# Attention with sixteen heads on one core: weighted sums two key blocks at a time, maxima from upper halves, and ScalarE's heads as straight code

## The reference

```python
xn = layernorm(x)
q = heads(xn @ q_w.T + q_b) / sqrt(16)
k = heads(xn @ k_w.T + k_b)
v = heads(xn @ v_w.T + v_b)
attn = softmax(einsum('bhqd,bhkd->bhqk', q, k))
ctx = einsum('bhqk,bhkd->bhqd', attn, v)
out = x + (merge(ctx) @ out_w.T + out_b) + ffn(xn)
```

## Time and profile before

| | |
|---|---|
| median of 3 runs | 2112.31 us (2112.14 to 2113.64) |
| the profiled execution's own time | 2113.7 us |
| its span, first to last instruction | 2111.9 us |
| mean granted TensorE clock | 0.993 |
| TensorE matmul busy | 2040.5 us (97%) |
| TensorE weight load busy | 689.0 us (33%) |
| ScalarE busy | 1939.8 us (92%) |
| VectorE busy | 319.3 us (15%) |
| DMA | 82.46 MB |

### The profile page before, as it was taken

How to read it: one execution, slowest core, us unless ns; L and a number is a source line. 1 busy time by engine, 2 the same in 40 slices (tenths; PEclk the granted TensorE clock), 3 DMA queues, 4 the chain that set the end, 5 groups by cost and what they waited for, 6 DMA issues and landing times.

```text
span 2111.9 us, 39181 instructions
## 1 busy us (share of the span) xinstructions
PE 2040.5 (97%) x13433; PEld 689.0 (33%) x13433; DVE 319.3 (15%) x798; ACT 1939.8 (92%) x2130; POOL 29.7 (1%) x53
## 2 busy tenths in 40 slices
PE   6889999999999999999999999999999999999988
PEld 4533333233333333323333333323333333223327
DVE  6531001010101001010101001010100101010106
ACT  2259999999999999999999999999999999999983
POOL 2000000000000000000000000000000000000000
PEclk9989999999999999999999999999999999999999
DMA  6960201111020211111020111112020111102022
GB/s 202 267 198 9 44 5 18 28 23 28 8 43 8 31 13 23 28 23 28 8 43 8 23 21 23 28 20 31 8 43 8 16 28 23 28 10 41 8 38 80
DMA packets 65569, 82.46 MB, mean 39 GB/s; under 512 B 9952, under 2 KB 47360, under 8 KB 62208
## 3 DMA queue, kind: packets, MB, share of 16 engines
q1 hardware_dynamic: 65472, 81.58, 18.9%
HBM read 54.79 MB, written 26.21 MB: 38 GB/s over the span
## 4 chain that ended last, share of the span: by engine, by line
PE 92%; ACT 2%; issue 2%; DMA 2%; SPq 1%; DVE 1%; ACTq 0%; DVEq 0%
PE banks L1001 47%; PE banks L988 38%; PE banks L949 2%; ACT probs L558 2%; PE banks L906 2%; PE banks L1100 1%; PE banks L917 1%; DMA k_parts<-probs 1%; PE banks L969 0%; PE banks L1084 0%; PE banks L1091 0%; DMA q_st<-q_parts 0%; PE banks L890 0%; DMA k_parts<-parts 0%; SPq L317 0%
## 5 line engine op out<-in xcount | busy, mean ns | idle before, releaser
L558 ACT ACTIVATE probs<-banks 128x1024 f32<-128x1024 f32 x2051 | 1890.0, 1282 | 33.4 <-PE banks L988 27.3
L1001 PE MATMUL banks<-probs,v_st 128*32 128x512 f32 x8192 | 1092.5, 605 | 0.0
L988 PE MATMUL banks<-q_st,k_st 50*128 50x512 f32 x4102 | 921.1, 484 | 28.8 <-ACT probs L558 25.9
L988 PEld LDWEIGHTS banks<-q_st,k_st 50*128 50x128 f32 x4102 | 379.1, 183 | 1046.2 <-ACT probs L558 1036.1
L1001 PEld LDWEIGHTS banks<-probs,v_st 128*32 128x32 f32 x8192 | 161.2, 108 | 277.7 <-issue 247.1
L745 DVE TENSOR_REDUCE mcol<-banks 128x8 f32<-128x512 f32 x66 | 45.6, 691 | 1042.3 <-PE banks L949 1042.3
L770 DVE STREAM_TRANSPOSE o_sb<-banks 128x512 f32<-128x512 f32 x32 | 22.9, 717 | 477.4 <-PE banks L1001 477.4
L949 PEld LDWEIGHTS banks<-k_st,q_st 48*128 48x128 f32 x528 | 69.5, 190 | 12.1 <-DMA q_st<-q_parts 8.3
L949 PE MATMUL banks<-k_st,q_st 48*128 48x64 f32 x528 | 65.2, 265 | 7.5 <-DMA q_st<-q_parts 7.5
L488 POOL COPY v_st<-v_all 128x256 f32 x32 | 12.8, 404 | 1788.8 <-PE banks L1001 1788.8
L518 ACT ACTIVATE parts<-banks,qk_bias 128x512 fp32r<-128x512 f32 x14 | 9.6, 687 | 30.8 <-PE banks L906 28.6
(11 more groups left out here) (80 smaller groups left out, 357.9 us busy)
## 6 DMA issues: line engine op xcount, KB each, us to landing
k_st<-k_parts SPq DMA_DIRECT2D x204, 128.0 KB, 4.3
q_st<-q_parts SPq DMA_DIRECT2D x204, 64.0 KB, 4.6
q_parts<-probs SPq DMA_DIRECT2D x9, 512.0 KB, 6.2
k_parts<-probs SPq DMA_DIRECT2D x9, 512.0 KB, 6.2
xnT_copy<-probs SPq DMA_DIRECT2D x8, 512.0 KB, 4.4
probs<-xnT_copy SPq DMA_DIRECT2D x8, 512.0 KB, 7.4
w_f<-xnT_copy SPq DMA_DIRECT2D x16, 256.0 KB, 4.6
out_dram<-qt SPq DMA_DIRECT2D x16, 256.0 KB, 2.1
```

What stands on the lines that cost most here:

```text
L558: act.activation(probs[:, at:at + wide * CHUNK].rearrange("p (t c) -> p t c", t=wide), banks[:, bank:bank + wide, :], ACT.Exp, scale=SCALE ...
L988: last = pe.matmul(banks[:, WIDE * (e % BUFS) + r - r0, :], k_mm[rows, kt * P:(kt + 1) * P], blocks[rows, qb // GROUPS], start=True, stop= ...
L1001: last = pe.matmul(banks[VCOLS * qb:VCOLS * (qb + 1), 6, :], v_st[:, kt, :], probs[:, at:at + CHUNK], start=(kt == 0), stop=(kt == KT - 1) ...
```

## The change

The exponentials of the first pass are written out for all 16 heads as straight code. The probes read only the upper 16 bits of the high parts of q and k, as bfloat16, in 16 rows instead of 48. The weighted sums of steps t - 1 and t are both issued at the last exponential of step t, for odd t only, so at every fourth exponential.

```diff
+        q_top, k_top = (t.bitcast(BF16).rearrange("p (c two) -> p c two", two=2)[:, :, 1] for t in (q_st, k_st))
...
-                with act.Fori(0, HEADS) as h:
-                    for e in range(HE):
-                        exps(h, e)
+                if c.full:
+                    with act.Fori(0, HEADS) as h:
+                        for e in range(HE):
+                            exps(h, e)
+                else:
+                    for h in range(HEADS):
+                        for e in range(HE):
+                            exps(h, e)
...
-                    rows = slice(j * GROUP, j * GROUP + KROWS)
+                    rows = slice(j * GROUP, j * GROUP + DH)
                     for i in range(JT):
                         at = u * UG + i * P
-                        last = pe.matmul(misc[:, i * AK:(i + 1) * AK], q_mm[rows, at:at + P], k_mm[rows, 0:AK],
+                        last = pe.matmul(misc[:, i * AK:(i + 1) * AK], q_top[rows, at:at + P], k_top[rows, 0:AK],
                                          start=True, stop=True)
...
-                        for t in range(STEPS):
+                        for t in range(1, STEPS, 2):
                             if exp_of(QB * t + QB - 1)[0] == e:
+                                weighted_sum(h, t - 1)
                                 weighted_sum(h, t)
```

## The result

The changed kernel takes 2203.27 us (median of 4 runs, 2202.97 to 2203.93) against 2112.22 for the kernel before: 91 us slower, a ratio of 1.0432 with a 95% interval of 1.0414 to 1.045. The forecast was 2217, the range 2188 to 2264.

What follows compares the result with a forecast made beforehand. ScalarE sets the pace, TensorE having 0.17 us to spare a step. The loop's 101.5, the start's 3 and the end's 0.9 make +105 us on 2113.7, 2219; the median is 1.4 lower, 2217; range 2188 to 2264.

Steps and rivals of the forecast that it cites:

- (a): In each group of four exponentials, the next pair of scores stands behind two sums: 3.94 us a group, +101.5 us.
- the block of two sums: TensorE's two sums in a row, from first sum to next pair of scores: 1.90 us, bounds 1.65 and 1.98.
- (b): At each head's end, ScalarE's branch goes: 25 us at most, already inside the group's time, so nothing more.
- (c): Probes for maxima on TensorE: 0.45 us each instead of 0.89, hidden in its idle time, costing nothing.
- The bound of 10 us: Cost over all heads if probes still take 0.89 us each and overshoot the free time: 10 us in all.
- (d): What waits for the sums (ring of 16 tiles, VectorE's transpose, GpSimd's copy of V): later by up to a step, none late.
- (e): Start and end of the pass: low clock for about a group, 3 us; second sum ahead of the last work, 0.9 us.
- The 0.9 us after the last group: At the pass's end, the second sum stands ahead of the last work: 0.9 us more.
- Rivals 1 and 2: Two sums fit the group, ScalarE sets the pace: 2074 us, 8%; or sets cost about 0.35, 3.74 a group: 2112, 3%.
- Rival 3: TensorE's idle in every group lowers the clock; if in a tenth of the groups, 147 us more, 2364; 2%.
- rival 4: bf16 probes shift the maxima; a flagged overflow runs the whole attention a second time, over 2000 us more; 1%.
- ScalarE's idle: Sign in the changed profile: idle before every fourth exponential, about 0.17 us, put down to the scores, some 85 us.

Runs made afterwards that it cites:

- The cut: Changed kernel with the second sum of each pair over 384 of 512 columns: 2093.27 us.
- the added work: Changed kernel with extra work of 256 columns between the two sums in 14 of 16 groups: 2485.81 us with four matmuls, 2481.96 with one.
- its move to another place: Changed kernel with the same extra matmuls ahead of the pair of scores that waits: 2342.97 us with four, 2338.06 with one.

## Why the prediction was right

The mechanism and its numbers held, point by point:

- **ScalarE, and not the 97% of TensorE, was the bound before.** Single sums with both other parts come to 2082, near ScalarE's floor, while TensorE is as busy as ever (97%).
- **(a) The loop.** Forecast 3.94 us a group, measured 3.91, and 512 x 0.03 = 15 us is about the whole distance from 2217 to 2203. The term that was too large is the block of two sums, "rounded up to 1.90": it takes 1.85, since the sets after the second cost 0.43 and not 0.45. The cut, the added work and its move to another place each changed the time, or the round, by about what the loop says (0.40 and 0.42 us a round for the 0.43 expected). One detail was off and cost nothing: the last two pairs follow each other more closely than 0.33, and the third then waits for ScalarE; TensorE's idle is 0.65 where 0.62 was forecast.
- **(b) Straight code** took the stall at a head's end away. That it adds nothing beyond the loop held for the sum, but was put badly: without it the same groups cost 33 us more, over the 25 that the prediction named as the most it could hold, so it was part of what kept the sum right.
- **(c) The probes** are hidden, even at 0.89 us. The bound of 10 us for that case was too high.
- **(d)** Nothing that waits for the sums was late.
- **(e)** 2008.9 us are 512 rounds (2001.9), two intervals (1.8) and 5 us more, where 3 had been set for the low clock at the start. The round of 4.14 us at each head's start, 0.23 more than the others, was not foreseen: 15 x 0.23 = 3.5 of the 5. The 0.9 us after the last group isn't there: from the start of the last exponential to the end are 59.2 us, and were 59.0. The pass also began 2.2 us earlier, for which nothing in the prediction stands. These small terms cancel, by luck, to within 1 us.

Rivals 1 and 2 fell with the round of 3.91. Rival 3 did not come about in this kernel (clock 1.00 in mid-kernel), but its mechanism is real: the clock does fall where TensorE idles longer, as after the branch of 6 us. The overflow of rival 4 did not occur: one pass of exponentials is in the trace.

Of the signs to look for, one was wrong: ScalarE's idle of 80.4 us (85 forecast) is put down to the scores by the profile in 7.9 us only, since it names a releaser for 16 of the waits and for most of the others none. The chain shows it better than the table of waits.

## What to carry to other kernels

When an engine is 97% busy and another 92%, lay a few periods side by side and ask which one waits where it is behind; the busy share alone named the wrong one here. Before putting two long pieces of work together, walk the loop of buffers: whatever stands between "buffer free" and "buffer filled again" is in the period, and work on the engine with time to spare is free in one place and paid in full in another. TensorE's branch back to the loop's start was cheap here only up to some size of the loop; look at a branch's duration after adding code.

## What the runs showed of the hardware

- TensorE's branch back over a head's code took 0.21 us with 802 matmul records in the loop and 6.02 us with 858 (medians). The Trainium skill (Runtime: NRT & Kernel Launch, Instruction fetch mechanics) says that a taken branch whose target has left the window of fetched code must wait for a fetch. The trace agrees: the instruction queue q8 moved 10 packets in the one and 146 in the other, and the step lies between these two sizes.
- ScalarE's loop costs reading too: queue q14 carried 87 instruction packets in the four kernels with ScalarE's loop, and 41 or 42 in all others, which have straight code.
- The clock fell to its lower level, 1.2 GHz, after TensorE had worked 2.75 of 7 us, and in the changed kernel with ScalarE's loop after 5.48 of 8 (640 to 648 us). It stayed at 1.00 (2.4 GHz) with 0.65 us of idle in each 3.91.
- Behind one set of four float32 matmuls over 32 columns each, a second starts 0.45 us later and each further one 0.43. The switch to the scores makes it 0.54. With 0.45 + 2 x 0.43 + 0.54 this is the 1.85 us of two sums.
